# The threshold search of a two-step graph attention layer: VectorE sums the part up to the threshold over a row with one padding column, and the one-element judgement and move lose their pointer scalars

## The chip, the cores and the metric

One core of one Trainium2 chip. The metric is the device time of one execution in microseconds. Nothing is moved between cores.

## The reference, cut to what matters

There are N = 3327 nodes with 256 features. The first layer runs two steps. In each, every row of attention is cut to its nucleus: the largest weights whose softmax mass reaches 0.9 are kept and rescaled.

```python
logits = Q @ W2 @ K.T / TAU
idx = jnp.argsort(-logits, axis=1)
vals = jnp.take_along_axis(logits, idx, axis=1)
csum = jnp.cumsum(jax.nn.softmax(vals, axis=1), axis=1)
k_i = jnp.sum(csum < P_NUC, axis=1) + 1
...
masked = jnp.where(keep, logits, -jnp.inf)
return jax.nn.softmax(masked, axis=1)
...
for s in range(STEPS):
    A = _adj_from_feats(Xa, W1, W2, W3)
    Xf = Rf @ Xf
    Xb = Rb @ Xb
    Xa = A @ Xa
    Z = Z + (Xf @ U1[s] + Xb @ U2[s] + Xa @ U3[s])
```

A layer norm and a second layer of masked edge attention follow. The change doesn't touch them.

## The kernel before, in words

The nodes lie in 26 tiles of 128 rows; a tile's attention is one buffer of 128 rows by NPAD = 3328 columns, of which the first N = 3327 are used. `phase_h` makes the projections, `layer_step` runs twice (step 0, step 1), then `phase_mid` and `phase_edges` do the rest.

In place of a sort, `layer_step` searches one threshold per row by bisection on a logarithmic scale, in BISECT = 19 rounds: sum the entries above `mid`, compare with the target 0.9 of the row's sum `Z`, and multiply `mid` by one of two factors. The tiles are taken in nine triples. Of the first eight, VectorE searches tiles r = 0 and r = 1 in alternation, and ScalarE searches r = 2 at the same time with a Sign pass (L673), a Relu pass (L679) and six short operations on single columns. The last triple (LAST) has two tiles: VectorE does tile 0 alone while ScalarE does the first 10 rounds of tile 1; then VectorE takes tile 1 over and does the other 9.

A round of a tile on VectorE has three parts. The **evaluation** (`evaluate`, L720; `alone`, L741; `go_on`, L758) is one scalar_tensor_tensor over the 3327 columns with `mid` as a pointer scalar, that is, one value per row read from memory, and the sum in `mass`; the accumulated sum is read out by a small instruction of its own. The **judgement** (`judge`, L727; L761 in `go_on`) works on one column: is `mass` at least `target` (a pointer scalar), times a constant, into `hit`. The **move** (`move`, L732; L764) also works on one column: (`hit` + constant) times `mid`, with the second `mid` as a pointer scalar. In the triples the order is written out by hand in beats, 38 for a triple; a beat is

```python
evaluate(g, it, r)
if it + r >= 1:
    move(g, it + r - 1, 1 - r)
judge(g, it, r)
between(g, 2 * it + r)
```

so the move of the other tile stands between a tile's evaluation and its judgement. The other work of VectorE is hung onto certain beats by `between`: it takes logits out of PSUM for the next triple (`take`, L699, 21 chunks in a triple that loads three tiles), finds their maxima (`highest`, L705), does the last tile's cut of the triple before (`cut`, L774), scales, row sums, and in step 0 the low parts of the projections (`low_parts`, L798 and L799). By its schedule 207 of the 304 beats of step 0 and 201 of the 304 of step 1 carry such work; the others are empty. In `alone` and `go_on` evaluation, judgement and move of one tile follow one another, each waiting for the one before.

ScalarE's program has beats of its own with fixed work: it evacuates transposes (L552), exponentiates the next triple's rows (L517), and in step 0 copies the mixed features (L584, L595, L606, L614). `begin` of VectorE waits for the exponents of its two tiles, `cut(g, 2)` for ScalarE's search, and `take_over` (L748) for ScalarE's tenth round in the last triple. TensorE runs in its own fixed order: logits (L909, L910) wait for `take` to free one of two banks, and transposes (L965) for the cuts and for ScalarE's evacuations. All waits are counted semaphores, also between instructions of one engine.

Of the kernel before, what the change touches and what calls it, by code (L numbers as in the profile page):

```python
# [7 lines left out]
ALU = mybir.AluOpType  # L8
# [3 lines left out]
BF16 = mybir.dt.bfloat16  # L12
# [3 lines left out]
P = 128  # L16
N = 3327
NT = -(-N // P)
NPAD = NT * P
# [10 lines left out]
P_NUC = 0.9  # L30
# [7 lines left out]
LAST = TRIPLES - 1  # L38
# [278 lines left out]
def roles(g):  # L317

    return [r for r in (0, 1, 2) if 3 * g + r < NT]
# [7 lines left out]
def home(g, r):  # L327

    return 3 * (g % 2) + (2 - r if g == LAST else (r + g // 2) % 3)


def rate(it):

    if it + 1 < BISECT:
        up = 2.0 ** (LOG_STEP / 2 ** (it + 1))
        return up, 1.0 / up
    return 1.0 - MARGIN, 2.0 ** (-LOG_STEP / 2 ** it) * (1.0 - MARGIN)


def layer_step(nc, sem_in, psum, sb_in, s, qk, s_op, a_op, env):  # L340
# [8 lines left out]
    tag = f"s{s}_"  # L349
# [31 lines left out]
    with ExitStack() as c:  # L381
        sb = sb_in(c)
        sem, cleared = sem_in(c)
        rows = sb(tag + "rows", [P, 6, NPAD], F32)
        dump = sb(tag + "dump", [P, N], BF16)
        adump = sb(tag + "adump", [P, N], I8)
        slab = sb(tag + "slab", [P, NSLAB, 7, P], F32)
        wT = sb(tag + "wT", [P, 2, CH], F32)
# [3 lines left out]
        nb, Z, target, mid, hit, mass, kept, rk = (  # L392
            sb(tag + n, [P, 6], F32) for n in ("nb", "Z", "target", "mid", "hit", "mass", "kept", "rk"))
# [29 lines left out]
        mass_done = [sem(f"{tag}mass{r}") for r in range(2)]  # L423
        begun, mid_ready, hit_ready = ([sem(f"{tag}{n}{r}") for r in range(2)] for n in ("begun", "mid", "hit"))

        def st(t, g, r):

            k = 3 * (g % 2) + r
            return t[:, k:k + 1]

        def row(g, r):
            return rows[:, home(g, r), 0:N]

        def w2d(ap):
            return ap.rearrange("(c p) n -> p c n", p=P)
# [254 lines left out]
        def _(dve):  # L690
# [15 lines left out]

            def begin(g, r):
                dve.wait_ge(S["exp_done"], LOADS.index((g, r)) + 1)
                nc.vector.tensor_scalar(st(target, g, r), st(Z, g, r), P_NUC, None, ALU.mult).then_inc(begun[r], 1)
                nc.vector.tensor_scalar(st(mid, g, r), st(Z, g, r), LEAST * 2.0 ** LOG_STEP, None, ALU.mult).then_inc(begun[r], 1)  # L710

            def evaluate(g, it, r):
                n = BISECT * g + it
                if it == 0:
                    dve.wait_ge(begun[r], 2 * (g + 1))
                else:
                    dve.wait_ge(mid_ready[r], n)
                if n + r >= 1:
                    dve.wait_ge(mass_done[1 - r], n + r)
                nc.vector.scalar_tensor_tensor(out=dump[:], in0=row(g, r), scalar=st(mid, g, r), in1=row(g, r),  # L720
                                               op0=ALU.is_gt, op1=ALU.mult, accum_out=st(mass, g, r)).then_inc(mass_done[r], 1)

            def judge(g, it, r):
                n = BISECT * g + it
                up, down = rate(it)
                dve.wait_ge(mass_done[r], n + 1)
                nc.vector.tensor_scalar(st(hit, g, r), st(mass, g, r), st(target, g, r), up - down, ALU.is_ge, ALU.mult).then_inc(hit_ready[r], 1)  # L727

            def move(g, it, r):
                n = BISECT * g + it  # L730
                dve.wait_ge(hit_ready[r], n + 1)
                nc.vector.tensor_scalar(st(mid, g, r), st(hit, g, r), rate(it)[1], st(mid, g, r), ALU.add, ALU.mult).then_inc(mid_ready[r], 1)  # L732

            def alone(it):
                n = BISECT * LAST + it
                if it == 0:
                    dve.wait_ge(begun[0], 2 * (LAST + 1))
                    dve.wait_ge(mass_done[1], n)
                else:
                    dve.wait_ge(mid_ready[0], n)  # L740
                nc.vector.scalar_tensor_tensor(out=dump[:], in0=row(LAST, 0), scalar=st(mid, LAST, 0), in1=row(LAST, 0),  # L741
                                               op0=ALU.is_gt, op1=ALU.mult, accum_out=st(mass, LAST, 0)).then_inc(mass_done[0], 1)
                judge(LAST, it, 0)
                move(LAST, it, 0)

            def take_over():
                dve.wait_ge(S["a_mid"], BISECT * LAST + FIRST_PART)
                nc.vector.tensor_scalar(st(target, LAST, 1), st(Z, LAST, 1), P_NUC, None, ALU.mult).then_inc(begun[1], 1)  # L748
                nc.vector.tensor_scalar(st(mid, LAST, 1), st(mid, LAST, 2), -1.0, None, ALU.mult).then_inc(mid_ready[1], 1)

            def go_on(it):
                n = BISECT * LAST + it - FIRST_PART
                up, down = rate(it)
                if it == FIRST_PART:
                    dve.wait_ge(begun[1], 2 * LAST + 1)
                    dve.wait_ge(mass_done[0], BISECT * TRIPLES)
                dve.wait_ge(mid_ready[1], n + 1)
                nc.vector.scalar_tensor_tensor(out=dump[:], in0=row(LAST, 1), scalar=st(mid, LAST, 1), in1=row(LAST, 1),  # L758
                                               op0=ALU.is_gt, op1=ALU.mult, accum_out=st(mass, LAST, 1)).then_inc(mass_done[1], 1)
                dve.wait_ge(mass_done[1], n + 1)  # L760
                nc.vector.tensor_scalar(st(hit, LAST, 1), st(mass, LAST, 1), st(target, LAST, 1), up - down,  # L761
                                        ALU.is_ge, ALU.mult).then_inc(hit_ready[1], 1)
                dve.wait_ge(hit_ready[1], n + 1)
                nc.vector.tensor_scalar(st(mid, LAST, 1), st(hit, LAST, 1), down, st(mid, LAST, 1), ALU.add, ALU.mult).then_inc(mid_ready[1], 1)  # L764

            def cut(g, r):
                f = 3 * g + r
                if r == 2:
                    dve.wait_ge(S["a_mid"], BISECT * (g + 1))
                elif (g, r) == (LAST, 1):  # L770
                    dve.wait_ge(mid_ready[1], BISECT * TRIPLES - FIRST_PART + 1)
                else:
                    dve.wait_ge(mid_ready[r], BISECT * (g + 1))
                nc.vector.scalar_tensor_tensor(out=row(g, r), in0=row(g, r), scalar=st(mid, g, r), in1=row(g, r),  # L774
                                               op0=ALU.is_gt, op1=ALU.mult,
                                               accum_out=kept[:, f % 6:f % 6 + 1]).then_inc(S["w_ready"], 1)

# [48 lines left out]
            def between(g, b):  # L826
                if g >= 1 and b == 2:
                    cut(g - 1, 2)
                if g >= 1 and b == 3:
                    for q in roles(g - 1):  # L830
                        scale(3 * (g - 1) + q)
                if s == 0 and g >= 1:
                    if b == 10:
                        row_sums(g - 1)
                    if b == 11:
                        row_rates(g - 1)
                    for q in roles(g - 1):
                        if b == TURN + STRIDE * q + 6:
                            low_parts(3 * (g - 1) + q)
                if s == 1 and g == 0:  # L840
                    for p in range(NPIECE):
                        if b == 2 + 3 * p:
                            scale_operand(p)
                if g + 1 < TRIPLES:
                    loads = len(roles(g + 1))
                    start = 35 - 9 * loads
                    for n in due(b - 1, start, 35, NCH * loads):
                        if n % NCH == NCH - 1:
                            highest(3 * (g + 1) + n // NCH)
                    for n in due(b, start, 35, NCH * loads):  # L850
                        take(3 * NCH * (g + 1) + n)

            for g in range(LAST):
                begin(g, 0)
                for it in range(BISECT):
                    for r in range(2):
                        if it == 0 and r == 1:
                            begin(g, 1)
                        evaluate(g, it, r)
                        if it + r >= 1:  # L860
                            move(g, it + r - 1, 1 - r)
                        judge(g, it, r)
                        between(g, 2 * it + r)
                cut(g, 0)
                move(g, BISECT - 1, 1)
                cut(g, 1)
# [747 lines left out]
```

## Time and profile before

| what | value |
|---|---|
| median of 3 runs | 3754.25 us (3752.21 to 3756.71) |
| the profiled execution | 3752.47 us |
| its span | 3750.6 us |
| its mean granted TensorE clock | 0.892 |
| VectorE busy | 3507.9 us, 94% |
| ScalarE busy | 3148.4 us, 84% |
| TensorE matmul busy | 2934.6 us, 78% |
| triples and last triple of step 0 | 70 to 1576 us |
| triples and last triple of step 1 | 1622 to 3115 us |
| the rest of the kernel | to 3750.6 us |

The span covers the instructions; the profiled execution's own time is 1.9 us longer. On VectorE and ScalarE the duration of an instruction overlaps the start of the next, so what an instruction costs is read from the distance between starts, not from its duration.

### The profile page before, as it was taken

How to read it: one execution, taken by the hardware profiler on the slowest of the kernel's cores; microseconds unless marked ns; L12 is line 12 of the kernel's file. 1: busy time of each engine (PE TensorE's matmuls, PEld its weight loads, DVE VectorE, ACT ScalarE, POOL GpSimd, SP SyncE). 2: the span in 40 equal slices, each digit the busy share in tenths (PEclk: the TensorE clock that was granted, in tenths of full speed). 3: DMA queues.
4: the chain of work that ended last, by engine and by line, in shares of the span. 5: the costliest groups of instructions: out<-in, count | busy, mean ns of one | idle time of the engine just before them, and what ended most of it. 6: DMA issues, size and time to landing. Idle time of an engine off the chain costs nothing. (4 is left out here: it accounts for less than half of the span.)

```text
span 3750.6 us, 42354 instructions
## 1 busy us (share of the span) xinstructions
PE 2934.6 (78%) x14004; PEld 2072.7 (55%) x14004; DVE 3507.9 (94%) x4688; ACT 3148.4 (84%) x4587; POOL 387.2 (10%) x457
## 2 busy tenths in 40 slices
PE   6568787787878788538879797978889754799998
PEld 4456666675757566413536354544536343567787
DVE  7999999999999999789999999999999995677887
ACT  6999999999999999479899999999999971344443
POOL 3000000000000000000000000000000002334444
PEclk9689888898989898769989898989999877999999
DMA  2112121312222220072121121212121103355563
GB/s 93 64 56 87 62 92 59 104 46 94 67 74 83 75 79 22 27 206 65 33 51 37 42 50 35 50 39 44 42 53 38 31 6 99 104 170 189 197 210 106
DMA packets 157020, 288.52 MB, mean 77 GB/s; under 512 B 14080, under 2 KB 93376, under 8 KB 153408
## 3 DMA queue, kind: packets, MB, share of 16 engines
q1 hardware_dynamic: 120400, 205.97, 17.7%
q10 hardware_dynamic: 21744, 62.79, 4.8%
q0 software_dynamic: 14656, 17.04, 3.3%
q8 instruction: 111, 1.82, 0.2%
q14 instruction: 109, 0.89, 0.1%
HBM read 232.80 MB, written 59.77 MB: 78 GB/s over the span
## 5 line engine op out<-in xcount | busy, mean ns | idle before, releaser
L720 DVE SCALAR_TENSOR_TENSOR s_dump<-s_rows,s_mid 128x3327 bf16<-128x3327 f32 x608 | 2238.5, 3682 | 2.3 <-issue 0.7
L673 ACT ACTIVATE s_adump<-s_rows,s_mid 128x3327 int8<-128x3327 f32 x324 | 995.1, 3071 | 10.5
L679 ACT ACTIVATE s_adump<-s_rows,s_mid 128x3327 int8<-128x3327 f32 x324 | 991.0, 3059 | 0.0
L932 PE MATMUL bank<-x,s_slab 128*128 128x512 f32 x1352 | 633.7, 612 | 0.0
L909 PE MATMUL bank<-kh,qs 128*128 128x512 f16 (+1 forms) x364 | 147.0, 404 | 379.6 <-DVE s_rows L699 369.5
L932 PEld LDWEIGHTS bank<-x,s_slab 128*128 128x128 f32 x1352 | 266.3, 198 | 280.3 <-issue 268.4
L976 PE MATMUL bank<-hb,s_wT 128*128 128x256 f32 x1352 | 358.4, 410 | 72.5 <-ACT s_wT L552 72.4
L976 PE MATMUL bank<-xab,s_wT 128*128 128x256 f32 x1352 | 349.1, 403 | 49.9 <-ACT s_wT L552 49.8
L965 PE MATMUL bank<-ident,s_rows 128*128 128x128 f32 x1352 | 231.3, 299 | 183.9 <-DVE s_rows L774 183.0
L932 PE MATMUL bank<-hb,s_slab 128*128 128x257 f32 x1352 | 351.0, 400 | 0.0
L976 PEld LDWEIGHTS bank<-hb,s_wT 128*128 128x128 f32 x1352 | 262.8, 205 | 123.1 <-ACT s_wT L552 55.9
L965 PEld LDWEIGHTS bank<-ident,s_rows 128*128 128x128 f32 x1352 | 188.5, 157 | 250.4 <-DVE s_rows L774 191.3
L976 PEld LDWEIGHTS bank<-xab,s_wT 128*128 128x128 f32 x1352 | 258.5, 202 | 93.0 <-ACT s_wT L552 42.3
L552 ACT ACTIVATE s_wT<-bank 128x512 f32<-128x512 f32 (+1 forms) x364 | 199.6, 550 | 127.9 <-PE bank L965 127.6
L909 PEld LDWEIGHTS bank<-kh,qs 128*128 128x128 f16 x364 | 42.9, 118 | 476.4 <-DVE s_rows L699 445.2
L932 PEld LDWEIGHTS bank<-hb,s_slab 128*128 128x128 f32 x1352 | 269.8, 202 | 60.2 <-issue 17.9
L1414 ACT ACTIVATE e_wh<-bank 128x512 f16<-128x512 f32 (+1 forms) x182 | 101.2, 565 | 202.0 <-PE bank L1546 201.6
L699 DVE TENSOR_SCALAR_CACHE_REDUCE s_rows<-bank 128x512 f32<-128x512 f32 (+1 forms) x364 | 232.7, 643 | 4.8 <-PE bank L910 3.4
L1363 POOL TENSOR_TENSOR e_rows<-e_rows,e_adj 128x3328 f32<-128x3328 f32 x25 | 181.2, 7247 | 233.2 <-ACT e_rows L1375 233.2
L937 PEld LDWEIGHTS bank<-hb,strip 128*128 128x128 f32 x1352 | 190.4, 197 | 13.2
L774 DVE SCALAR_TENSOR_TENSOR s_rows<-s_rows,s_mid 128x3327 f32<-128x3327 f32 x52 | 191.4, 3680 | 0.9
L494 POOL COPY qs<-s_q 64x128 f16<-64x128 f16 x26 | 32.5, 1249 | 1516.6 <-ACT s_q L618 1516.6
(183 smaller groups left out, 4824.2 us busy)
## 6 DMA issues: line engine op xcount, KB each, us to landing
s_slab<-adjT_dram SPq DMA_DIRECT2D x104, 448.0 KB, 3.9
s_slab<-adjT_dram SPq DMA_DIRECT2D x104, 384.0 KB, 3.7
e_adj<-adjR_dram ACTq DMA_DIRECT2D x23, 1664.0 KB, 7.2
strip<-adjR_dram SPq DMA_DIRECT2D x52, 448.0 KB, 3.5
strip<-adjR_dram SPq DMA_DIRECT2D x52, 384.0 KB, 3.3
e_ring<-sc_d SPq DMA_DIRECT2D x72, 256.0 KB, 5.4
sc_d<-e_stage SPq DMA_DIRECT2D x60, 256.0 KB, 2.4
su_d<-s_su_out ACTq DMA_DIRECT2D x26, 256.0 KB, 2.0
```

The costliest lines, as they stand in the source:

```text
L552: nc.scalar.activation(wT[:, n % 2, 0:w], bank_of("quad", n)[:, 0:w], ACT.Copy).then_inc(S["ev_done"], 1)
L673: nc.scalar.activation(adump[:], row(g, r), ACT.Sign, bias=st(mid, g, 2), accum_out=cnt[:]).then_inc(S["a_eval"], 1)
L679: nc.scalar.activation(adump[:], row(g, r), ACT.Relu, bias=st(mid, g, 2), accum_out=gap[:]).then_inc(S["a_eval"], 1)
L699: nc.vector.tensor_scalar(rows[:, home(g, r), ch * CH:ch * CH + w], psL[n % 2][:, 0:w], 1.0, None, ALU.mult, ALU.max, accum_out=mx[:, home ...
L720: nc.vector.scalar_tensor_tensor(out=dump[:], in0=row(g, r), scalar=st(mid, g, r), in1=row(g, r), op0=ALU.is_gt, op1=ALU.mult, accum_out=s ...
L774: nc.vector.scalar_tensor_tensor(out=row(g, r), in0=row(g, r), scalar=st(mid, g, r), in1=row(g, r), op0=ALU.is_gt, op1=ALU.mult, accum_out ...
L909: nc.tensor.matmul(psL[n % 2][:, 0:w], lhs, kh2[:, cols], start=True, stop=False)
L932: ins = nc.tensor.matmul(acc, slab[:, i % NSLAB, j - PIECES[p], :], s_op[:, j, 0:SN], start=False, stop=(j == NT - 1))
L937: ins = nc.tensor.matmul(psS[t % 2][:, SN + j:SN + j + 1], strip[:, i % 2, k * P:(k + 1) * P], s_op[:, 0, D:SN], start=False, stop=(j == N ...
L965: ins = nc.tensor.transpose(bank[:, k * P:(k + 1) * P], rows[:, home(g, r), j * P:(j + 1) * P], ident[:])
L976: ins = nc.tensor.matmul(psA[f % 2][:, 0:D], wT[:, n % 2, k * P:(k + 1) * P], a_op[:, j, 0:D], start=(j == 0), stop=(j == NT - 1))
L1363: nc.gpsimd.tensor_tensor(em[:, t % 3], em[:, t % 3], adj[:, t % 3], ALU.mult).then_inc(S["w_ready"], 1)
```

## The change

VectorE sums the part up to the threshold, no longer the part above it. The padding column of a row that VectorE searches is set to `Z` times (0.9 - 1), so the sum of the part up to `mid`, padding included, is compared with 0.0. `target` is no longer written or read by VectorE. The move becomes a scalar_tensor_tensor with `mid` as its second tensor and the factor as a constant. The judgement goes behind the beat's other work. The evaluation and the cut run over 3328 columns. ScalarE's search is the same.

```diff
-        dump = sb(tag + "dump", [P, N], BF16)
+        dump = sb(tag + "dump", [P, NPAD], BF16)
...
+        def wide_row(g, r):
+            return rows[:, home(g, r), :]
+
+        def rest(g, r):
+            return rows[:, home(g, r), N:NPAD]
...
             def begin(g, r):
                 dve.wait_ge(S["exp_done"], LOADS.index((g, r)) + 1)
-                nc.vector.tensor_scalar(st(target, g, r), st(Z, g, r), P_NUC, None, ALU.mult).then_inc(begun[r], 1)
+                nc.vector.tensor_scalar(rest(g, r), st(Z, g, r), P_NUC - 1.0, None, ALU.mult).then_inc(begun[r], 1)
...
-                nc.vector.scalar_tensor_tensor(out=dump[:], in0=row(g, r), scalar=st(mid, g, r), in1=row(g, r),
-                                               op0=ALU.is_gt, op1=ALU.mult, accum_out=st(mass, g, r)).then_inc(mass_done[r], 1)
+                nc.vector.scalar_tensor_tensor(out=dump[:], in0=wide_row(g, r), scalar=st(mid, g, r), in1=wide_row(g, r),
+                                               op0=ALU.is_le, op1=ALU.mult, accum_out=st(mass, g, r)).then_inc(mass_done[r], 1)
...
-                nc.vector.tensor_scalar(st(hit, g, r), st(mass, g, r), st(target, g, r), up - down, ALU.is_ge, ALU.mult).then_inc(hit_ready[r], 1)
+                nc.vector.tensor_scalar(st(hit, g, r), st(mass, g, r), 0.0, up - down, ALU.is_le, ALU.mult).then_inc(hit_ready[r], 1)
...
-                nc.vector.tensor_scalar(st(mid, g, r), st(hit, g, r), rate(it)[1], st(mid, g, r), ALU.add, ALU.mult).then_inc(mid_ready[r], 1)
+                nc.vector.scalar_tensor_tensor(out=st(mid, g, r), in0=st(hit, g, r), scalar=rate(it)[1], in1=st(mid, g, r),
+                                               op0=ALU.add, op1=ALU.mult).then_inc(mid_ready[r], 1)
...
                         evaluate(g, it, r)
                         if it + r >= 1:
                             move(g, it + r - 1, 1 - r)
+                        between(g, 2 * it + r)
                         judge(g, it, r)
-                        between(g, 2 * it + r)
```

`alone`, `take_over`, `go_on` and `cut` are changed in the same way: wide rows and `is_le` in the evaluations, wide rows in the cut, no pointer scalar in judgement and move, the padding cell in place of the target.

## Rows read from the trace of the kernel before

**Rows 1.** The page, part 1: busy time, share and instructions of each engine.
```profile
PE 2934.6 (78%) x14004; PEld 2072.7 (55%) x14004; DVE 3507.9 (94%) x4688; ACT 3148.4 (84%) x4587; POOL 387.2 (10%) x457
```

**Rows 2.** Timeline of VectorE, step 0: start, duration; an empty beat's end, then a filled one's.
```profile
716.47 0.21 DVE L732 TENSOR_SCALAR s_mid<-s_hit,s_mid 128x1 f32<-128x1 f32 x1
716.59 0.21 DVE L727 TENSOR_SCALAR s_hit<-s_mass,s_target 128x1 f32<-128x1 f32 x1
716.72 3.68 DVE L720 SCALAR_TENSOR_TENSOR s_dump<-s_rows,s_mid 128x3327 bf16<-128x3327 f32 x1
...
720.32 0.21 DVE L732 TENSOR_SCALAR s_mid<-s_hit,s_mid 128x1 f32<-128x1 f32 x1
720.45 0.21 DVE L727 TENSOR_SCALAR s_hit<-s_mass,s_target 128x1 f32<-128x1 f32 x1
720.57 0.68 DVE L699 TENSOR_SCALAR_CACHE_REDUCE s_rows<-bank 128x512 f32<-128x512 f32 x1
```

**Rows 3.** Timeline of VectorE, the last triple of step 1, one round of a tile alone.
```profile
3047.42 0.09 DVE L741 DVE_READ_ACCUMULATOR s_dump<-s_rows,s_mid 128x1 f32 x1
3047.54 0.21 DVE L727 TENSOR_SCALAR s_hit<-s_mass,s_target 128x1 f32<-128x1 f32 x1
3047.79 0.21 DVE L732 TENSOR_SCALAR s_mid<-s_hit,s_mid 128x1 f32<-128x1 f32 x1
3048.04 3.69 DVE L741 SCALAR_TENSOR_TENSOR s_dump<-s_rows,s_mid 128x3327 bf16<-128x3327 f32 x1
```

**Rows 4.** Timeline of VectorE, the begin of the first triple of step 0.
```profile
70.14 0.14 DVE L709 TENSOR_SCALAR s_target<-s_Z 128x1 f32<-128x1 f32 x1
70.20 0.14 DVE L710 TENSOR_SCALAR s_mid<-s_Z 128x1 f32<-128x1 f32 x1
70.38 3.69 DVE L720 SCALAR_TENSOR_TENSOR s_dump<-s_rows,s_mid 128x3327 bf16<-128x3327 f32 x1
```

**Rows 5.** Groups of VectorE's instructions by shape: busy us, mean ns; idle before.
```profile
L720 DVE SCALAR_TENSOR_TENSOR s_dump<-s_rows,s_mid 128x3327 bf16<-128x3327 f32 x608 | 2238.5, 3682 | 2.3 <-issue 0.7
...
L732 DVE TENSOR_SCALAR s_mid<-s_hit,s_mid 128x1 f32<-128x1 f32 x646 | 135.2, 209 | 1.3
L727 DVE TENSOR_SCALAR s_hit<-s_mass,s_target 128x1 f32<-128x1 f32 x646 | 133.8, 207 | 1.9
...
L1434 DVE TENSOR_SCALAR e_pen<-e_adj 128x1024 bf16<-128x1024 f32 x52 | 41.4, 800 | 0.0
...
L1434 DVE TENSOR_SCALAR e_pen<-e_adj 128x1279 bf16<-128x1279 f32 x26 | 21.5, 828 | 0.0
...
L1492 DVE TENSOR_TENSOR e_rows<-e_rows,e_adj 128x3328 f32<-128x3328 f32 x1 | 3.6, 3627 | 2.3 <-ACT e_rows L1375 2.3
```

**Rows 6.** Timeline of ScalarE and VectorE at the take-over in step 0.
```profile
1531.07 0.39 ACT L544 ACTIVATE s_mid<-s_sgn,s_mean,s_fac 128x1 f32<-128x1 f32 x1
...
1531.49 0.15 DVE L748 TENSOR_SCALAR s_target<-s_Z 128x1 f32<-128x1 f32 x1 [0.97 <-ACT s_mid L544]
```

**Rows 7.** ScalarE's waits in step 0, from 73.6 to 1532 us: total us, times, longest.
```profile
ACT s_wT L552 <- PE bank L965: 14.5, 13, 2.7
ACT s_su_out L595 <- PE bank L996: 9.3, 8, 2.2
```

**Rows 8.** Timeline of TensorE in step 0, its longest idle stretch near 704 us.
```profile
703.96 0.61 PE L909 MATMUL bank<-kh,qs 128*128 128x512 f16 x1 [6.03 <-DVE s_rows L699]
```

**Rows 9.** ScalarE's third exponent for triple 2, and VectorE's begin that needs it.
```profile
402.09 0.20 ACT L517 ACTIVATION_READ_ACCUMULATOR s_rows<-s_rows,s_nb 128x1 f32 x1
...
413.33 0.14 DVE L709 TENSOR_SCALAR s_target<-s_Z 128x1 f32<-128x1 f32 x1
```

**Rows 10.** Timeline of ScalarE and VectorE at the take-over in step 1.
```profile
3069.02 0.39 ACT L544 ACTIVATE s_mid<-s_sgn,s_mean,s_fac 128x1 f32<-128x1 f32 x1
...
3072.98 0.14 DVE L748 TENSOR_SCALAR s_target<-s_Z 128x1 f32<-128x1 f32 x1
```

**Rows 11.** ScalarE's waits in step 1, from 1625.2 to 3070 us: total us, times, longest.
```profile
ACT s_wT L552 <- PE bank L965: 36.1, 30, 4.8
```

More of the change, by code:

```diff
@@ L740, in alone @@
                     dve.wait_ge(mid_ready[0], n)
-                nc.vector.scalar_tensor_tensor(out=dump[:], in0=row(LAST, 0), scalar=st(mid, LAST, 0), in1=row(LAST, 0),
-                                               op0=ALU.is_gt, op1=ALU.mult, accum_out=st(mass, LAST, 0)).then_inc(mass_done[0], 1)
+                nc.vector.scalar_tensor_tensor(out=dump[:], in0=wide_row(LAST, 0), scalar=st(mid, LAST, 0), in1=wide_row(LAST, 0),
+                                               op0=ALU.is_le, op1=ALU.mult, accum_out=st(mass, LAST, 0)).then_inc(mass_done[0], 1)
                 judge(LAST, it, 0)
@@ L747, in take_over @@
                 dve.wait_ge(S["a_mid"], BISECT * LAST + FIRST_PART)
-                nc.vector.tensor_scalar(st(target, LAST, 1), st(Z, LAST, 1), P_NUC, None, ALU.mult).then_inc(begun[1], 1)
+                nc.vector.tensor_scalar(rest(LAST, 1), st(Z, LAST, 1), P_NUC - 1.0, None, ALU.mult).then_inc(begun[1], 1)
                 nc.vector.tensor_scalar(st(mid, LAST, 1), st(mid, LAST, 2), -1.0, None, ALU.mult).then_inc(mid_ready[1], 1)
@@ L757, in go_on @@
                 dve.wait_ge(mid_ready[1], n + 1)
-                nc.vector.scalar_tensor_tensor(out=dump[:], in0=row(LAST, 1), scalar=st(mid, LAST, 1), in1=row(LAST, 1),
-                                               op0=ALU.is_gt, op1=ALU.mult, accum_out=st(mass, LAST, 1)).then_inc(mass_done[1], 1)
+                nc.vector.scalar_tensor_tensor(out=dump[:], in0=wide_row(LAST, 1), scalar=st(mid, LAST, 1), in1=wide_row(LAST, 1),
+                                               op0=ALU.is_le, op1=ALU.mult, accum_out=st(mass, LAST, 1)).then_inc(mass_done[1], 1)
                 dve.wait_ge(mass_done[1], n + 1)
-                nc.vector.tensor_scalar(st(hit, LAST, 1), st(mass, LAST, 1), st(target, LAST, 1), up - down,
-                                        ALU.is_ge, ALU.mult).then_inc(hit_ready[1], 1)
+                nc.vector.tensor_scalar(st(hit, LAST, 1), st(mass, LAST, 1), 0.0, up - down, ALU.is_le, ALU.mult).then_inc(hit_ready[1], 1)
                 dve.wait_ge(hit_ready[1], n + 1)
-                nc.vector.tensor_scalar(st(mid, LAST, 1), st(hit, LAST, 1), down, st(mid, LAST, 1), ALU.add, ALU.mult).then_inc(mid_ready[1], 1)
+                nc.vector.scalar_tensor_tensor(out=st(mid, LAST, 1), in0=st(hit, LAST, 1), scalar=down, in1=st(mid, LAST, 1),
+                                               op0=ALU.add, op1=ALU.mult).then_inc(mid_ready[1], 1)
             def cut(g, r):
@@ L773, in cut @@
                     dve.wait_ge(mid_ready[r], BISECT * (g + 1))
-                nc.vector.scalar_tensor_tensor(out=row(g, r), in0=row(g, r), scalar=st(mid, g, r), in1=row(g, r),
+                nc.vector.scalar_tensor_tensor(out=wide_row(g, r), in0=wide_row(g, r), scalar=st(mid, g, r), in1=wide_row(g, r),
                                                op0=ALU.is_gt, op1=ALU.mult,
```

## The prediction

> **What bounds the kernel now.** I read the busy times first, then VectorE's groups by shape, then its timeline beat by beat, and last what ScalarE waits for. The busy times show VectorE at 94% of the span and ScalarE at 84% [rows 1]. The groups show where VectorE's time is: 608 evaluations with 2.3 us of idle before all of them together, and the judgements and moves, 646 each, with 1.3 and 1.9 us [rows 5]. So in the two steps VectorE waits for nobody; it is the bound there, and what a beat loses on it, the span can lose. The exception is the last triple of step 0: at the take-over VectorE sat 0.97 us until ScalarE's tenth round was done [rows 6]. That row decides how much of the gain arrives, as worked out below.
>
> **What a one-element instruction costs.** The durations of about 208 ns [rows 5] overlap what follows, so I go by starts. In a beat the move starts at 716.47, the judgement at 716.59, the next evaluation at 716.72 [rows 2]: each takes 0.125 us of VectorE. Both have a pointer scalar. The nearest instruction without one is the target of `begin`: it starts at 70.14 and the next at 70.20 [rows 4], 0.06 us; I take 0.065. Taking away a pointer scalar thus gives back 0.06 us where nothing else holds the next instruction. Where the next one needs the result, it starts 0.25 us after an instruction with a pointer (3047.54 to 3047.79, and again to 3048.04 [rows 3]) and 0.18 after one without (70.20 to 70.38 [rows 4]): 0.065 us given back there.
>
> The judgement loses its pointer and stays a tensor_scalar, so the row of `begin` prices it directly. The move becomes a scalar_tensor_tensor with two one-element tensors, and no row shows that. Bounds: 0.06 us as in `begin`, or 0.125 us as now, if the second tensor costs what the pointer did. The two-tensor instruction over 3328 columns takes 3627 ns, the evaluation with its pointer over 3327 takes 3682 [rows 5]: the pointer is 55 ns dearer than a second tensor with none. I take 0.065 us.
>
> **The beats.** A filled beat has other work behind the judgement (720.32, 720.45, 720.57 [rows 2]). After the change the order is move, other work, judgement, next evaluation. Nothing needs a result that is late there, so both instructions give back their share: 0.12 us. The judgement goes behind the takes and so behind their wait for TensorE, but its result is first read by the move behind the next evaluation, 3.6 us later; nothing is lost.
>
> An empty beat is different. The judgement needs the sum that the evaluation left, and starts 0.12 us after the start of the accumulator's read-out even with nothing in front of it (3047.42 to 3047.54 [rows 3]). In the beat it starts at the same 0.12 us, and the move lies in that gap (716.47 to 716.59 [rows 2]). A shorter move gives nothing there: the judgement starts at 0.12, and then takes 0.065. The next evaluation needs the move's result, which is there 0.18 us after the move's start. Both come to 0.185 against 0.25: 0.065 us given back, not 0.12.
>
> Step 0: 207 filled beats x 0.12 = 24.8 us and 97 empty ones x 0.065 = 6.3. Between the two cuts of each of the eight triples stands a move on which the second cut waits: 8 x 0.065 = 0.5. Tile 0 of the last triple is searched alone, with judgement and move both in the chain: 19 x 0.13 = 2.5. Sum up to the take-over 34.1. Step 1: 201 x 0.12 = 24.1, 103 x 0.065 = 6.7, 0.5 and 2.5, sum 33.8. Behind the take-over nine rounds with judgement and move in the chain: 9 x 0.13 = 1.2 us in each step.
>
> **What it adds.** One more column in 304 evaluations, 24 cuts and 19 evaluations alone, in each step, up to the take-over. A column is 3682 / 3327 = 1.1 ns [rows 5], so 347 x 1.1 = 0.4 us per step. The write of the padding cell takes the place of the write of the target, one element each: nothing. `is_le` for `is_gt` is another comparison in the same place: nothing. No DMA, no queue and no instruction of another engine is moved. VectorE offers 33.7 us up to the take-over of step 0 and 33.4 us up to that of step 1.
>
> **Whether ScalarE lets it through.** ScalarE's program is unchanged. In step 0 it has next to no slack at the end: its tenth round in the last triple ends at 1531.46 and VectorE, there 1 us before, starts at 1531.49 [rows 6]. So step 0 can end earlier only by as much as ScalarE gets there earlier, and that is by the waits it loses. Before that take-over they are 14.5 us for transposes and 9.3 us for mixed features [rows 7], together 23.8 us; shorter kinds may add about 1 to 2. Are these waits VectorE's doing? Mostly: TensorE, which is named as the releaser, sat idle 6.03 us before it until VectorE had freed a bank, and only then came to the mixing for which ScalarE waited [rows 8]. When VectorE runs 4 us earlier per triple, such waits close. I leave 1.5 us of them to TensorE's own work: 22.3 us arrive of the 33.7 offered. The rest, 11.4 us, becomes a new wait of VectorE for ScalarE, first at the take-over of step 0, or at the low parts two rounds ahead of it. It does not come sooner: the third exponent of a triple is done at 402.2 and VectorE asks for it at 413.33 [rows 9], 11 us of room, which the gap between 31 us offered by the eighth triple and some 20 taken by ScalarE only just uses up.
>
> In step 1 ScalarE has more room. At the take-over it is done 3.6 us before VectorE asks (3069.41 against 3072.98 [rows 10]), and it has 36.1 us of waits for transposes behind it [rows 11]; it must lose 33.4 - 3.6 = 29.8 of these. They hang on VectorE's cuts and banks in the same way, so I take the full 33.4 us.
>
> **Sum.** Step 0: 22.3 + 1.2 = 23.5 us. Step 1: 33.4 + 1.2 = 34.6 us. Together 58.1 us off the profiled execution's 3752.5: 3694.4 us, which I give as 3694. That execution was 1.8 us under the median of the three runs, so against the median the same gain gives 3696; a difference inside the spread of the runs. A measurement of this kernel can tell about 0.2%, 7.5 us, from no change.
>
> **The rivals.**
>
> *The whole of VectorE's gain arrives.* If ScalarE's waits go entirely and its rounds are a little shorter for some reason, step 0 gives 33.7 + 1.2 + the 0.97 of its present wait, 35.9, and step 1 34.6: 70.5 us, 3682 us. Against it: all waits in [rows 7] together fall 10 us short of what is needed. Chance 0.07.
>
> *The move is no cheaper.* If a second tensor costs what the pointer did (the upper bound above), a filled beat gives back 0.06 only, an empty one still 0.065, a chained round 0.065: 12.4 + 6.3 + 1.2 + 0.6 - 0.4 = 20.1 us in step 0 and 12.1 + 6.7 + 1.2 + 0.6 - 0.4 = 20.2 in step 1, 3712 us, and ScalarE is not in the way. For it: no row shows the instruction. Against it: the 55 ns between the two wide instructions. Chance 0.15.
>
> *ScalarE gives back only half of its waits,* because TensorE's own work stands behind the others. Step 0 then gives 11.9 + 1.2 and step 1 18 + 3.6 + 1.2: 36 us, 3716 us. For it: TensorE is 78% busy [rows 1], and each wait names it. Against it: its idle time ends with VectorE's takes [rows 8]. Chance 0.1.
>
> *No change.* If a one-element instruction cost its place in the queue whatever its operands, the edit would give back nothing and the columns would add 0.8 us: 3753 us. Against it stand the 0.06 us of `begin` beside the 0.125 us of judgement and move, two starts apart [rows 2, 4]. Chance 0.04. The Trainium skill states such a rule: "VectorE: DVE Perf Modes", section "Rules for kernel authors", says of chained operations that the drain happens regardless and that one should minimize the count of operations; the count here stays the same, so by that rule there is nothing to gain. The starts just cited don't agree with it, since instructions of one size differ by a factor of two.
>
> *Slower.* The place is the evaluation: the count of columns goes from odd to even, and 664 of them make up most of VectorE's time. Two shapes of one instruction in the last phase show that a rate per column can differ: 1024 columns take 800 ns and 1279 take 828 [rows 5]. With 160 ns of fixed time taken off both, that is 0.625 against 0.52 ns a column; 0.1 ns over 3328 columns is 0.35 us per evaluation, 232 us in all, and with VectorE's 70 us of gain the kernel would take about 3915 us. It decides from 58 us / 664 = 0.09 us per evaluation on. Against it: the even two-tensor instruction of 3328 columns runs at the same rate as the odd evaluation [rows 5]. Chance 0.04.
>
> **How the numbers follow.** The forecast has the remaining 0.60. Its own range is 3686 (all of ScalarE's waits go, the starts are each 5 ns better) to 3703 (a third of step 0's waits stay). The range is to hold 8 in 10: down to 3684 it takes in most of what lies between the forecast and the first rival; up to 3714 it takes in the unchanged move and most of the halved waits. Left out are the whole gain at its best, no change, slower, and part of the halved waits, under 0.2. Faster by over 0.2% are the forecast and the first three rivals, 0.92; I say 0.91. Within 0.2%: 0.05. Slower: 0.04.
>
> **What the profile after would show.** Judgement and move at about 145 to 150 ns each, not 208. In the timeline of an empty beat 0.18 to 0.19 us from the read-out's start to the next evaluation, and 0.12 to the judgement; in a filled one 0.06 from the move to the other work, and 0.06 from the judgement to the evaluation. The evaluation 1 to 2 ns longer, no more. ScalarE's waits for transposes and mixed features in step 0 down from 23.8 to some 2 us, and a new wait of VectorE for ScalarE of about 10 us in the last triple of step 0, at the take-over or at the low parts; none in step 1. A move near 208 ns would mean the second rival; waits of ScalarE for TensorE that stay above 10 us in step 0 the third; an evaluation 90 ns longer the last. Should VectorE wait in step 1 as well, I have overrated what ScalarE can give there.

## The result, and the profile after

The changed kernel takes 3702.24 us (median of 4 runs, 3701.07 to 3703.32) against 3753.57 us before (4 runs): ratio 0.9862, 95% interval 0.9847 to 0.9876. The profiled execution takes 3701.07 us, 51.4 less than that of before. A second set of runs of the same kernel gave 3706.27 us (3704.31 to 3708.65), ratio 0.9874 (0.9857 to 0.989). The forecast was 3694 us, with a range of 3684 to 3714. The last phases took what they took before (639.3 and 639.0 us from the start of the last cut to the end), so all of the gain lies in the two steps.

The page of the kernel after, part 1, answers to [rows 1]; below it the groups of VectorE's instructions by shape, which answer to [rows 5].

```profile
PE 2920.7 (79%) x14004; PEld 2065.5 (56%) x14004; DVE 3446.8 (93%) x4688; ACT 3145.3 (85%) x4587; POOL 408.9 (11%) x457
```

```profile
L726 DVE SCALAR_TENSOR_TENSOR s_dump<-s_rows,s_mid 128x3328 bf16<-128x3328 f32 x608 | 2236.9, 3679 | 2.1 <-issue 0.8 <-DVE s_mid L716 0.2
L705 DVE TENSOR_SCALAR_CACHE_REDUCE s_rows<-bank 128x512 f32<-128x512 f32 x312 | 212.6, 685 | 11.7 <-PE bank L917 10.3
...
L738 DVE SCALAR_TENSOR_TENSOR s_mid<-s_hit,s_mid 128x1 f32<-128x1 f32 x646 | 101.9, 158 | 1.3
L733 DVE TENSOR_SCALAR s_hit<-s_mass 128x1 f32<-128x1 f32 x646 | 96.9, 150 | 2.5
```

The judgement (L733) is down from 207 ns to 150, the move (L738) from 209 to 158. The evaluation (L726) with its additional column is not longer. The idle time ahead of the takes (L705) has grown: 10.3 us of it is for TensorE, against 3.4 us before, and the 6.9 us that are new lie in step 1.

The timeline of VectorE shows a filled beat's end (717.01 to 717.76), an empty one's (729.25 to 729.45), and then, near 3015 us, a chained round. These answer to [rows 2, 3].

```profile
717.01 0.08 DVE L726 DVE_READ_ACCUMULATOR s_dump<-s_rows,s_mid 128x1 f32 x1
717.01 0.15 DVE L738 SCALAR_TENSOR_TENSOR s_mid<-s_hit,s_mid 128x1 f32<-128x1 f32 x1
717.08 0.69 DVE L705 TENSOR_SCALAR_CACHE_REDUCE s_rows<-bank 128x512 f32<-128x512 f32 x1
717.69 0.08 DVE L705 DVE_READ_ACCUMULATOR s_rows<-bank 128x1 f32 x1
717.69 0.15 DVE L733 TENSOR_SCALAR s_hit<-s_mass 128x1 f32<-128x1 f32 x1
717.76 3.67 DVE L726 SCALAR_TENSOR_TENSOR s_dump<-s_rows,s_mid 128x3328 bf16<-128x3328 f32 x1
...
729.25 0.08 DVE L726 DVE_READ_ACCUMULATOR s_dump<-s_rows,s_mid 128x1 f32 x1
729.25 0.15 DVE L738 SCALAR_TENSOR_TENSOR s_mid<-s_hit,s_mid 128x1 f32<-128x1 f32 x1
729.37 0.15 DVE L733 TENSOR_SCALAR s_hit<-s_mass 128x1 f32<-128x1 f32 x1
729.45 3.69 DVE L726 SCALAR_TENSOR_TENSOR s_dump<-s_rows,s_mid 128x3328 bf16<-128x3328 f32 x1
...
3014.36 0.08 DVE L748 DVE_READ_ACCUMULATOR s_dump<-s_rows,s_mid 128x1 f32 x1
3014.48 0.15 DVE L733 TENSOR_SCALAR s_hit<-s_mass 128x1 f32<-128x1 f32 x1
3014.67 0.16 DVE L738 SCALAR_TENSOR_TENSOR s_mid<-s_hit,s_mid 128x1 f32<-128x1 f32 x1
3014.86 3.69 DVE L748 SCALAR_TENSOR_TENSOR s_dump<-s_rows,s_mid 128x3328 bf16<-128x3328 f32 x1
```

Between the starts, an instruction without a pointer scalar takes 0.07 us. In the empty beat the judgement still begins 0.12 us after the start of the read-out, and the evaluation 0.20. A chained round's overhead is down from 0.62 us to 0.50.

At the take-over of step 0 ScalarE and VectorE show this (it answers to [rows 6]):

```profile
1504.88 0.39 ACT L550 ACTIVATE s_mid<-s_sgn,s_mean,s_fac 128x1 f32<-128x1 f32 x1
...
1505.29 0.15 DVE L755 TENSOR_SCALAR s_rows<-s_Z 128x1 f32<-128x1 f32 x1 [3.80 <-ACT s_mid L550]
```

What ScalarE waited for, first in step 0 up to there, then in step 1 up to its take-over, and what VectorE waited for in step 1 (the same views as [rows 7, 11]; us in total, times, longest). `s_wT` is ScalarE's evacuation of the transposes, `s_rows L705` VectorE's take of the logits:

```profile
ACT s_wT L558 <- PE bank L972: 1.5, 3, 1.0
...
ACT s_wT L558 <- PE bank L972: 20.7, 22, 3.0
...
DVE s_rows L705 <- PE bank L917: 6.9, 7, 2.2
```

In step 0 the waits for mixed features (9.3 us) are gone altogether and those for transposes are down from 14.5 to 1.5. In step 1 over half of ScalarE's waits stay, and VectorE has one that it had not. ScalarE's room at the take-over of step 1, 3.6 us before [rows 10], is used up too: its tenth round ends at 3022.89, and VectorE goes on at 3022.92.

| stretch, from the first evaluation of the step | before | after | gain | forecast |
|---|---|---|---|---|
| step 0 to the take-over | 1461.1 | 1434.8 | 26.3 | 22.3 |
| step 0, take-over to last cut | 41.6 | 40.5 | 1.1 | 1.2 |
| step 1 to the take-over | 1451.0 | 1428.2 | 22.8 | 33.4 |
| step 1, take-over to last cut | 38.4 | 37.3 | 1.0 | 1.2 |

### The profile page after: what moved, and what is told of

Same layout as the page of the kernel before. It is cut to its first block and busy times, and to the rows that moved or that the text cites. A ratio compares the mean times of both kernels' runs of the same rounds, so it can differ in the third digit from the quotient of the medians.

```text
span 3699.3 us, 42354 instructions
## 1 busy us (share of the span) xinstructions
PE 2920.7 (79%) x14004; PEld 2065.5 (56%) x14004; DVE 3446.8 (93%) x4688; ACT 3145.3 (85%) x4587; POOL 408.9 (11%) x457
## 5 line engine op out<-in xcount | busy, mean ns | idle before, releaser
L726 DVE SCALAR_TENSOR_TENSOR s_dump<-s_rows,s_mid 128x3328 bf16<-128x3328 f32 x608 | 2236.9, 3679 | 2.1 <-issue 0.8
L939 PE MATMUL bank<-hb,s_slab 128*128 128x257 f32 x1352 | 361.7, 409 | 0.0
L983 PEld LDWEIGHTS bank<-hb,s_wT 128*128 128x128 f32 x1352 | 254.6, 199 | 171.3 <-ACT s_wT L558 84.9
L705 DVE TENSOR_SCALAR_CACHE_REDUCE s_rows<-bank 128x512 f32<-128x512 f32 (+1 forms) x364 | 233.8, 647 | 11.7 <-PE bank L917 10.3
L500 POOL COPY qs<-s_q 64x128 f16<-64x128 f16 x26 | 53.5, 2058 | 1468.2 <-ACT s_q L624 1468.2
L781 DVE SCALAR_TENSOR_TENSOR s_rows<-s_rows,s_mid 128x3328 f32<-128x3328 f32 x52 | 191.4, 3681 | 0.7
```

Of the source, the lines that this page charges most:

```text
L705: nc.vector.tensor_scalar(rows[:, home(g, r), ch * CH:ch * CH + w], psL[n % 2][:, 0:w], 1.0, None, ALU.mult, ALU.max, accum_out=mx[:, home ...
L726: nc.vector.scalar_tensor_tensor(out=dump[:], in0=wide_row(g, r), scalar=st(mid, g, r), in1=wide_row(g, r), op0=ALU.is_le, op1=ALU.mult, a ...
L781: nc.vector.scalar_tensor_tensor(out=wide_row(g, r), in0=wide_row(g, r), scalar=st(mid, g, r), in1=wide_row(g, r), op0=ALU.is_gt, op1=ALU. ...
L939: ins = nc.tensor.matmul(acc, slab[:, i % NSLAB, j - PIECES[p], :], s_op[:, j, 0:SN], start=False, stop=(j == NT - 1))
L983: ins = nc.tensor.matmul(psA[f % 2][:, 0:D], wT[:, n % 2, k * P:(k + 1) * P], a_op[:, j, 0:D], start=(j == 0), stop=(j == NT - 1))
```

## The experiments

All times in us; the kernel before ran beside each (medians 3753.55 to 3754.23).

| run | median | ratio to before, interval |
|---|---|---|
| judge_pointer | 3728.70 | 0.9934 (0.9919 to 0.9949) |
| move_pointer | 3723.50 | 0.9921 (0.9906 to 0.9935) |
| old_order | 3716.10 | 0.9901 (0.9885 to 0.9918) |
| width_only | 3754.80 | 1.0003 (0.9993 to 1.0012) |
| act_extra_after | 3718.25 | 0.9906 (0.9889 to 0.9922) |
| act_extra_before | 3753.66 | 1.0000 (0.9990 to 1.0009) |
| sweep_light | 3695.19 | 0.9843 (0.9828 to 0.9857) |
| logits_early | 3709.99 | 0.9883 (0.9868 to 0.9898) |
| sweeps_late | 3696.23 | 0.9845 (0.9830 to 0.9859) |
| after_again | 3706.27 | 0.9874 (0.9857 to 0.9890) |

### What the pointers and the order are worth

**The judgement with a pointer.**

```diff
-                nc.vector.tensor_scalar(st(hit, g, r), st(mass, g, r), 0.0, up - down, ALU.is_le, ALU.mult).then_inc(hit_ready[r], 1)
+                nc.vector.tensor_scalar(st(hit, g, r), st(mass, g, r), nil[:], up - down, ALU.is_le, ALU.mult).then_inc(hit_ready[r], 1)
```

> The changed kernel, but the judgement compares with a pointer scalar (a column that holds zero). Theory (a pointer scalar costs VectorE some 0.05 us between starts, and the judgement lies on its path in every beat): 608 x 0.05 and 56 x 0.06 in the chained rounds come back, some 34 us; the 3.8 us that VectorE now waits at the take-over of step 0 and part of the 6.9 us for which it waits for TensorE in step 1 take some of it up: 3725 to 3733 us. Rival (a one-element instruction costs the same whatever its operands, and the gain came from the order): 3702 us.

Measured was 3728.70, as the theory has it.

**The move with a pointer.**

```diff
-                nc.vector.scalar_tensor_tensor(out=st(mid, g, r), in0=st(hit, g, r), scalar=rate(it)[1], in1=st(mid, g, r),
-                                               op0=ALU.add, op1=ALU.mult).then_inc(mid_ready[r], 1)
+                nc.vector.tensor_scalar(st(mid, g, r), st(hit, g, r), rate(it)[1], st(mid, g, r), ALU.add, ALU.mult).then_inc(mid_ready[r], 1)
```

> The changed kernel, but the move is the old tensor_scalar with a pointer scalar. Theory (in an empty beat the move is hidden under the judgement's wait for the sum, so only the 408 filled beats and the 56 chained rounds pay): 408 x 0.05 + 56 x 0.06 = 24 us, less 4 us of the wait at the take-over and up to 7 us of waits for TensorE: 3714 to 3722 us, and in empty beats the judgement still 0.12 us behind the read-out. Rival (each of the 664 moves pays): 3725 to 3733 us, like the judgement's pointer.

Measured was 3723.50, between the two: 1.5 us above the theory's range, 1.5 below the rival's. The beats below say why.

**The judgement ahead of the other work.**

```diff
-                        between(g, 2 * it + r)
                         judge(g, it, r)
+                        between(g, 2 * it + r)
```

> The changed kernel, but with the judgement ahead of the beat's other work, as before. Theory (in filled beats the judgement then waits 0.12 us for the sum, and the shorter move gives nothing there either): 408 x 0.04 = 16 us come back on VectorE, of which the 3.8 us at the take-over and up to 7 us of waits for TensorE take up a part: 3708 to 3715 us. Rival (the order is worth nothing): 3702 us.

Measured was 3716.10, a little beyond the theory. With both pointers gone, the order is worth some 10 to 14 us (against the 3706.27 and the 3702.24 of the changed kernel).

For these kernels I took from the timelines the time from the start of an evaluation's read-out to the start of the next evaluation, less the take between them, as a mean over the 175 empty beats that lie between two evaluations and the 295 beats that hold one take (those of them with a recorded wait left out):

| kernel | empty beat, us | beat with one take, us |
|---|---|---|
| before | 0.250 | 0.253 |
| after | 0.198 | 0.140 |
| judge_pointer | 0.249 | 0.200 |
| move_pointer | 0.244 | 0.194 |
| old_order | 0.200 | 0.194 |
| width_only | 0.249 | 0.251 |

In a filled beat, in the new order, either pointer costs 0.055 to 0.06. In the old order both together cost no more than that (0.253 against 0.194), and without pointers the order is worth 0.054. No run has both pointers in the new order; if they add up, it would show 0.25, like the kernel before, and the order alone would have gained nothing. In an empty beat the pointers don't add up: either alone brings the whole 0.25 us back. There are two chains side by side from the read-out to the next evaluation. One is the sum's 0.12 us, and then the judgement's place, 0.12 with a pointer and 0.07 without. The other is the move's result, 0.25 or 0.20 us after its start. The longer of the two counts, so in the empty beats one edit without the other would have been worth next to nothing (0.249 and 0.244 against 0.250). That is what the theory on move_pointer had left out: it saw the move hidden under the sum, and not that the evaluation waits for it. The order is worth nothing in an empty beat (0.200 against 0.198).

### The additional column

```diff
-                nc.vector.scalar_tensor_tensor(out=dump[:], in0=row(g, r), scalar=st(mid, g, r), in1=row(g, r),
+                nc.vector.scalar_tensor_tensor(out=dump[:], in0=wide_row(g, r), scalar=st(mid, g, r), in1=wide_row(g, r),
```

> The kernel before, with evaluations and cuts over 3328 columns in place of 3327 and nothing else changed. Theory (one more column costs nothing that can be seen, as the changed kernel's starts suggest): 3753.5 to 3754.5 us, with 3.60 us from an evaluation's start to its read-out as before. Rival (the even count makes an evaluation shorter or longer by several ns, and part of the result is this): 5 ns each way are 3 us, 3750 or 3757.

Measured was 3754.80, ratio 1.0003: no change that can be told from noise. Its group of evaluations:

```profile
L723 DVE SCALAR_TENSOR_TENSOR s_dump<-s_rows,s_mid 128x3328 bf16<-128x3328 f32 x608 | 2237.1, 3679 | 2.3 <-issue 0.7
```

3679 ns against 3682 for one column less [rows 5]. The distance from an evaluation's start to its read-out is 3.604 us on the mean in the kernel before, 3.606 here and 3.604 in the changed kernel. So the other rate that the rival supposed, 90 ns an evaluation and more, is not there. Whether one column costs the 1.1 ns that I had added, 0.7 us in all, these runs cannot tell.

### Who sets the end of step 0

```diff
                 nc.scalar.activation(mean[:], st(mid, g, 2), ACT.Copy, scale=last * (down + up) / 2).then_inc(S["a_fac"], 1)
+                if s == 0:
+                    nc.scalar.activation(spare[:], st(mid, g, 2), ACT.Copy, scale=1.0)
```

In the changed kernel:

> The changed kernel with one more one-column copy per round on ScalarE, in step 0 only (162 copies into a cell that nobody reads, each about 0.1 us between starts: some 15 us of ScalarE). Theory (since the change ScalarE sets the end of step 0's search, and has no wait left to give): 13 to 16 us longer, 3715 to 3718 us, and VectorE's waits for ScalarE in step 0 about 18 us. Rival (VectorE is still the bound, and its wait at the take-over is incidental): 0 to 5 us longer, 3702 to 3707.

In the kernel before:

> The kernel before with the same extra copies on ScalarE in step 0. Theory (there ScalarE had 25 us of waits that VectorE caused): they take up the 15 us, 0 to 3 us longer, 3753 to 3757 us. Rival (ScalarE was on the path of step 0 before as well, as the wait at the take-over hints): 10 to 15 us longer, 3764 to 3769.

The changed kernel took 16.0 us more than its first set of runs (3718.25; 12.0 more than its second), the kernel before nothing (3753.66; ratio 1.0000). The profiles put this into step 0: up to the take-over it takes 1451.0 us where it took 1434.8, and step 1 takes 1428.7 where it took 1428.2. Both theories hold: before, ScalarE had 15 us to give in step 0; since the change it has none. VectorE's waits in step 0 of act_extra_after (`kl` is the low parts, `s_rows L758` the take-over, `s_rows L708` a take):

```profile
DVE kl L808 <- ACT s_q L627: 11.9, 14, 1.6
DVE s_rows L758 <- ACT s_mid L553: 7.0, 1, 7.0
DVE s_rows L708 <- PE bank L920: 0.8, 1, 0.8
```

With ScalarE slower still, VectorE meets it in the low parts of many triples, 14 times, and at the take-over for the rest.

This also corrects a reading. In the kernel before with ScalarE's additional 15 us, the wait at the take-over is what it was [rows 6]:

```profile
1532.21 0.15 DVE L751 TENSOR_SCALAR s_target<-s_Z 128x1 f32<-128x1 f32 x1 [0.98 <-ACT s_mid L547]
```

So that wait of about 1 us didn't mean that ScalarE had no room. The kernel before has this on TensorE and VectorE ahead of the take-over:

```profile
1522.07 0.29 DVE L799 TENSOR_TENSOR qs<-bank,s_q 64x128 f16<-64x128 f32 x1
...
1522.51 2.05 PE L996 MATMUL bank<-s_u,s_xT 128*128 128x512 f32 x2 [12.33 <-DVE qs L799]
```

TensorE sat 12.3 us until VectorE's low parts, placed in its eighteenth round, freed a bank, then mixed the features that ScalarE had to copy within its last round (it waited 1.35 us for them), and VectorE arrived 1 us before ScalarE was through. VectorE waited for a chain that it had started itself.

### Where step 1's gain went

**Less work on TensorE.**

```diff
-                for j in blocks:
+                for j in (blocks if s == 0 else blocks[-1:]):
                     ins = nc.tensor.matmul(acc, slab[:, i % NSLAB, j - PIECES[p], :], s_op[:, j, 0:SN], start=False, stop=(j == NT - 1))
```

> The changed kernel without most of step 1's sweep matmuls: of each half only its last block is multiplied, so the swept parts of step 1 are not computed. Theory (TensorE's own work in step 1 makes its logits late): VectorE's 6.9 us of waits for logits go, and ScalarE's waits for transposes fall from 21 us to under 10; 3694 to 3697 us. Rival (TensorE only passes on that ScalarE is behind, since it waits for ScalarE's evacuations ahead of the logits): the waits of VectorE stay, 3700 to 3703 us.

Measured was 3695.19, as the theory has it in time and in VectorE's waits. Step 1 to its take-over takes 1420.4 us, 30.6 less than before, and VectorE has no wait for TensorE left in it. ScalarE's waits for transposes fall to 12.4 us, not under 10.

**The logits one beat earlier.**

```diff
-                        for n in due(b, 34 - 9 * loads, 34, NCH * loads):
+                        for n in due(b, 34 - s - 9 * loads, 34 - s, NCH * loads):
                             logits(3 * NCH * (g + 1) + n)
```

> The changed kernel with TensorE's logits of step 1 one beat earlier in its order. Theory (VectorE's waits come from the place of the logits in TensorE's order): they go, 3695 to 3698 us. Rival (TensorE then waits for VectorE's banks ahead of the transposes, and ScalarE gets these later): 3702 to 3712 us, with longer waits of ScalarE for transposes in step 1.

Measured was 3709.99, in the rival's range, which an edit without effect would have met as well; what decides are its waits, and step 1 to its take-over, 1435.9 us against 1428.2. The waits in its step 1 (`s_rows L755` is the take-over):

```profile
DVE s_rows L705 <- PE bank L917: 10.0, 10, 3.0
DVE s_rows L755 <- ACT s_mid L550: 4.4, 1, 4.4
...
ACT s_wT L558 <- PE bank L972: 28.2, 22, 8.6
```

TensorE's order is shared: logits put forward make transposes late, ScalarE falls behind, and VectorE waits for both.

**The sweeps later.**

```diff
+        if s == 1 and 0 < g < LAST:
+            return [HALVES * g + h for h in due(b, 3, 22, 9)] + [HALVES * g + 9 + h for h in due(b, 22, BEATS - 1, HALVES - 9)]
```

> The changed kernel with step 1's sweeps moved in TensorE's order: of the 26 halves of a triple only 9 (before: 14) in the beats 3 to 21, where transposes and attention run too, and 17 behind them. All work is done. Theory (TensorE is behind in those beats by its own work, and VectorE waits for its logits near beat 23): VectorE's 6.9 us of waits go, and 3694 to 3697 us. Rival (the logits are late for another reason, or the sweeps are missed later, by ScalarE): 3700 to 3706 us.

Measured was 3696.23, with all of the work done, against 3706.27 for the changed kernel on the same chip, as the theory has it; each of its four runs (3695.28 to 3697.01) is shorter than any of the eight of the changed kernel. Its waits in step 1, VectorE's (all that there are) and ScalarE's:

```profile
DVE s_dump L728 <- issue: 0.8, 3, 0.3
...
ACT s_wT L560 <- PE bank L974: 13.0, 15, 4.8
```

Step 1 to its take-over takes 1420.5 us, as in sweep_light. Only the place of TensorE's own matmuls was changed, so VectorE's new wait came from TensorE being behind by its own work. In the changed kernel it shows as follows, TensorE first:

```profile
2696.99 1.88 PE L936 MATMUL bank<-s_u,s_xT 128*128 128x512 f32 x4
2698.71 2.74 PE L939 MATMUL bank<-x,s_slab 128*128 128x512 f32 x6
2701.28 0.38 PE L916 MATMUL bank<-kh,qs 128*128 128x512 f16 x1
...
2701.91 0.69 DVE L705 TENSOR_SCALAR_CACHE_REDUCE s_rows<-bank 128x512 f32<-128x512 f32 x1 [2.22 <-PE bank L917]
```

VectorE's move has started at 2699.55 and the logits begin only at 2701.28, behind a sweep; TensorE shows no idle time from 2655 on. This version is faster than both kernels: 0.9845 (0.9830 to 0.9859) of before.

**The changed kernel once more.**

> The changed kernel once more, on the same chip as its neighbour: 3701 to 3704 us; VectorE's wait at the take-over of step 0 between 3.8 and 5.4 us, its waits for logits in step 1 near 7 us.

Measured was 3706.27, 2 us above what was expected; in its profile VectorE waits 8.3 us for logits in step 1 and 5.2 us at the take-over of step 0, against 6.9 and 3.8.

## Why the prediction was right, and where its terms were off

The time lies in the range and the gain is 51 us where 58 were forecast. It is so near partly by luck: step 0 gave 4 us more than its sum, step 1 some 11 us less, and the two errors offset each other in part. The signs in the profile that the prediction named came as follows.

**The starts: right in kind, a little too good.** I took 0.065 us for an instruction without a pointer; the median is 0.066 for the judgement ahead of an evaluation and 0.072 for the move ahead of a take. Filled beats give back 0.113 us (forecast 0.12), empty ones 0.052 (0.065), chained rounds 0.12 (0.13). That the empty beat gives about half was right, and so was the reason that both chains end there together.

**VectorE's offer: 33.7 and 33.4 us forecast, about 29 and 31 measured.** Step 0: 26.3 us arrived, and the wait at the take-over grew from 1.0 to 3.8, so 29.1 were offered. Step 1: 30.6, read from sweep_light. In step 0 about 1.8 us of the difference lie in 20 beats in which low parts stand right behind the move: 0.16 us pass between the two starts, not 0.072, and the move itself lasts 0.24 us there, not 0.15 to 0.16. In move_pointer 0.13 us pass, in judge_pointer 0.07 in all but two; what makes this difference is open.

**"22.3 us arrive of the 33.7 offered" in step 0: the mechanism right, both sizes off.** ScalarE is what ends the search now (act_extra_after), and its waits went. Of the two kinds that I had summed, 1.5 us stayed, just what I had left to TensorE, so they gave the 22.3. The other 4.0 us of the 26.3 are what the sum lacked: a third wait of ScalarE for TensorE, ahead of its copies in L606, 1.5 us before and gone after, and some 2.4 us by which ScalarE's own instructions and the short gaps between them got shorter, for which I have no cause. The new wait was 3.8 us and not some 10, since the offer was smaller and the passage larger. The step from the 1 us wait at the take-over to "next to no slack" was wrong for the kernel before, as act_extra_before shows. It did no harm to the sum, because the sum was made from ScalarE's waits, and these were its slack.

**"So I take the full 33.4 us" in step 1: the term that failed.** 22.8 us arrived. Of the 10.6 missing, 2.8 are the starts and 7.8 are the new wait: 6.9 us recorded for logits, the rest not laid to a row. I had asked only whether ScalarE would let the gain through and priced TensorE's lateness at 1.5 us in step 0 and at nothing in step 1. ScalarE was not free to pass it on either: I had said that it must lose 29.8 us, and its tenth round came only 19.3 us earlier from the first evaluation on, which with its 3.6 us of room is the 22.8 that arrived. So in this profile both engines reach the take-over together, and which of the two would have held the other is not separated. In after_again ScalarE is done 1.6 us ahead and VectorE's waits are what counts. With the sweeps spread, ScalarE's waits fell to 13.0 us and VectorE's went, so one cause stands behind both: TensorE's own work. The third rival had that work behind ScalarE's waits, and its sum for step 1 up to the take-over, 21.6 us, comes near; that VectorE itself would wait for logits it did not have. TensorE was busy with matmuls for 139.46 of the 169.0 us of such a triple (the stretch from 2603.2 to 2772.2 us of the changed kernel, one row of the busy times by stretch; the columns are matmuls, weight loads, VectorE, ScalarE and GpSimd, then the granted clock, the DMA engines' busy share and GB/s):

```profile
2603.20:2772.20 169.00, 139.46 (x462) 80.09 (x462) 166.66 (x210) 166.17 (x235) 7.71 (x9) 0.92 0.18 44
```

That is 83% with room on the mean, but none in the beats in which transposes, attention, logits and sweeps meet.

**The rivals.** The unchanged move is refuted by 158 ns and 0.072 us. No change is refuted by the changed kernel itself and by the runs with a pointer: VectorE has 4688 instructions in the kernels before and after and in move_pointer, and two more in judge_pointer, and the times are 3754, 3702, 3724 and 3729 us. The rule that the Trainium skill states for chained operations ("VectorE: DVE Perf Modes", "Rules for kernel authors") is thus not the whole of it here: operands count too. Slower is refuted by width_only. The halved waits of ScalarE came true in step 1 only (36.1 us [rows 11] to 20.7). That the whole of VectorE's gain arrives did not come true in either step.

## What to carry to other kernels

For a short instruction ask for the distance between starts, and follow every chain to the next long instruction separately: an edit on one of two equal chains is worth nothing, on both it is worth the difference. Shorter instructions and a better order can need each other in the same way: in a filled beat of the old order the two pointers together were worth 0.059 us, in the new order either of them is. When one engine gets faster by 2%, look at every engine that it feeds or drains, in the stretch where the work meets and not over the span: here ScalarE took up 3 us of the 29 offered in one step and TensorE's order 8 of the 31 in the other, and the latter came back when TensorE's sweeps were spread. A wait for an engine at one point does not show that this engine has no room; adding a known cost to it does.

## What was not expected of the hardware

One column more in a two-tensor instruction of 3327 columns did not lengthen it by anything that could be measured (3682 ns, then 3679; from start to read-out 3.604 us in both kernels). A scalar_tensor_tensor on one column with a constant takes 158 ns, 8 more than a tensor_scalar with constants (150), and with a pointer scalar the tensor_scalar takes 207. And the same kernel differed between two sets of runs by 4 us (3702.24 and 3706.27), in its profiles, which lie 3.2 us apart, mostly by its waits for other engines (3.8 and 6.9 us of VectorE's, then 5.2 and 8.3), not by any instruction.
